# AdaLN FFN on one core: tile 2's experts through ScalarE and VectorE, tile 3's blocks through GpSimd, three convolutions in a row, input 3 issued without a wait

## The reference, cut to what matters

```python
att = softmax(gelu(gelu(c @ W0 + b0) @ W1 + b1) @ W2 + b2)        # 32 x 8
agg_w = einsum('bk,koi->boi', att, weight)                        # one 128x128 matrix per tile
y = einsum('boi,bih->boh', agg_w, x) + (att @ bias_k)[:, :, None] # the "convolution"
qg, sg = dynamic_quant(y * inv_gate); qu, su = dynamic_quant(y * inv_up)   # by row maximum
gate = (qg @ w_gate.T) * sg * s_wgate; up = (qu @ w_up.T) * su * s_wup     # 2048 -> 1024
inter = clip(silu(gate) * up, -10, 10)
qi, si = dynamic_quant(inter * inv_inter)
out = x + (qi @ w_down.T) * si * s_wdown                          # 1024 -> 2048
```

## Time and profile before

| | us |
|---|---|
| median of 3 runs | 804.18 |
| the profiled execution's own time | 804.37 |
| its span in the trace | 802.6 |
| TensorE busy with matmuls | 793.7 |
| VectorE busy | 716.2 |
| ScalarE busy | 441.0 |
| GpSimd busy | 146.1 |

### The profile page before, as it was taken

The page is one execution under the profiler, slowest core; times in us unless marked ns, Lnnn a source line. Parts: engine busy times, 40 slices in busy tenths (PEclk is TensorE's granted clock), DMA queues, the critical chain, the costliest instruction groups (busy, mean ns, idle before and its releaser), DMA issues.

```text
span 802.6 us, 9187 instructions
## 1 busy us (share of the span) xinstructions
PE 793.7 (99%) x3521; PEld 365.1 (45%) x3521; DVE 716.2 (89%) x810; ACT 441.0 (55%) x385; POOL 146.1 (18%) x138
## 2 busy tenths in 40 slices
PE   8999999999999999999999999999999999999997
PEld 4554444444444444444444444444444444444443
DVE  6987899999888998888998888998888988888968
ACT  6774335556664545654555654555654546655531
POOL 2603210210122220122220222210222210222000
PEclk9999999999999999999999999999999999999999
DMA  9997745554445444445444455445455544354342
GB/s 298 241 216 154 163 135 179 146 170 124 127 145 171 145 145 123 120 151 169 146 145 118 118 158 164 150 145 111 120 163 159 156 136 128 107 168 153 94 108 105
DMA packets 162964, 119.81 MB, mean 149 GB/s; under 512 B 151780, under 2 KB 152164, under 8 KB 153703
## 3 DMA queue, kind: packets, MB, share of 16 engines
q1 hardware_dynamic: 161192, 106.64, 44.7%
q0 software_dynamic: 1728, 12.58, 7.7%
HBM read 60.48 MB, written 33.55 MB: 117 GB/s over the span
## 4 chain that ended last, share of the span: by engine, by line
PE 91%; DVE 6%; ACT 2%; issue 1%; DMA 0%; DVEq 0%; ACTq 0%
PE gate_ps L614 26%; PE up_ps L614 26%; PE down_ps L717 23%; PE conv_ps L567 12%; DVE amax L1093 1%; PE gate_ps L717 1%; ACT y L810 0%; DVE region L1165 0%; PE down_ps L572 0%; DVE down_sc L1257 0%; DVE xt L1266 0%; DVE part_max L1172 0%; PE conv_ps L572 0%; ACT wd L810 0%; DVE region L1111 0%
## 5 line engine op out<-in xcount | busy, mean ns | idle before, releaser
L717 PE MATMUL down_ps<-wd,qiT 128*128 128x512 bf16 x896 | 211.2, 379 | 0.0
L614 PE MATMUL gate_ps<-wg,qgT 128*128 128x512 bf16 x928 | 205.7, 379 | 0.0
L614 PE MATMUL up_ps<-wu,quT 128*128 128x512 bf16 x896 | 202.4, 379 | 0.0
L1093 DVE TENSOR_REDUCE amax<-region 128x1 f32<-128x2048 f32 (+1 forms) x90 | 173.1, 1923 | 1.2
L442 POOL TENSOR_TENSOR prod<-wexp,att_bc 128x1024 f32<-128x1024 f32 x28 | 53.1, 1896 | 540.2 <-DVE region L1151 498.5
L717 PEld LDWEIGHTS down_ps<-wd,qiT 128*128 128x128 bf16 x896 | 87.5, 98 | 123.4 <-issue 29.1
L614 PEld LDWEIGHTS gate_ps<-wg,qgT 128*128 128x128 bf16 x928 | 90.7, 98 | 109.5 <-issue 1.1
L614 PEld LDWEIGHTS up_ps<-wu,quT 128*128 128x128 bf16 x896 | 87.7, 98 | 106.1 <-ACT quT L886 0.4
L821 ACT ACTIVATE qg<-region,recip 128x2048 f16<-128x2048 f32 x30 | 60.1, 2002 | 128.3 <-DVE recip L1103 128.3
L567 PE MATMUL conv_ps<-xt,aggw 128*128 128x512 f32 x244 | 116.3, 599 | 1.4 <-ACT y L810 0.8
L810 ACT ACTIVATE y<-conv_ps,aggb 128x512 bf16<-128x512 f32 x116 | 78.9, 686 | 60.0 <-PE conv_ps L567 55.4
(11 more groups left out here) (180 smaller groups left out, 581.2 us busy)
## 6 DMA issues: line engine op xcount, KB each, us to landing
xt<-x SPq DMA_DIRECT2D x30, 1024.0 KB, 4.8
out<-xt SPq DMA_DIRECT2D x29, 1024.0 KB, 4.0
wg<-w_gateT POOLq DMA_DIRECT2D x4, 1024.0 KB, 20.5
wu<-w_upT POOLq DMA_DIRECT2D x4, 1024.0 KB, 17.2
wd<-w_downT POOLq DMA_DIRECT2D x4, 1024.0 KB, 8.6
xt<-x SPq DMA_DIRECT2D x4, 512.0 KB, 4.7
invg_bc<-inv_gate SPq DMA_DIRECT2D x1, 1024.0 KB, 8.7
out<-xt SPq DMA_DIRECT2D x2, 512.0 KB, 2.9
```

Of the source, the lines that this page charges most:

```text
L614: last = nc.tensor.matmul(acc[:, n * BANK:(n + 1) * BANK], codes[:, k * P:(k + 1) * P], wts[:, k, n * BANK:(n + 1) * BANK], start=(k == 0) ...
L717: last = nc.tensor.matmul(down_bank(t, c), qiT_at(t)[:, k * P:(k + 1) * P], wd[:, k, c * BANK:(c + 1) * BANK], start=(k == ks[0]), stop=(k ...
L1093: nc.vector.tensor_reduce(amax[:, i:i + 1], src, axis=AX.X, op=ALU.max, apply_absolute_value=True).then_inc(max_ready, 1)
```

## The change

Tile 2's matrix is no longer made by TensorE. ScalarE writes eight scaled experts into `prod2` (in the place of the up weights' second chunk, which is not loaded yet), spread between its evictions of conv(0) and one after them, and VectorE adds them pairwise in three operations in the middle of `quant_first`. Tile 3's identity blocks now come from GpSimd, in the place where tile 2's came from. On TensorE conv(2) follows conv(1) at once and conv(3) comes before turn_g(1). Tile 3's result gets a home of its own (`quT`), ScalarE's and VectorE's orders are changed to match, and SyncE's wait ahead of x[3] is gone. The diff, cut to its core:

```diff
@@ homes, banks
-        Y_HOME = [y[:, :], wd_part(0, bf16), wd_part(1, bf16)]
+        Y_HOME = [y[:, :], wd_part(0, bf16), wd_part(1, bf16), quT[:, :]]
-            return Y_HOME[t] if t < EARLY else y[:, :]
+            return Y_HOME[t] if t <= EARLY else y[:, :]
-            return bank(up_ps, c - 2) if t < EARLY and c >= 2 else bank(conv_ps, c % 2)
+            return bank(up_ps, c - 2) if t <= EARLY and c >= 2 else bank(conv_ps, c % 2)
+        prod2 = wu[:, 4:6, :].rearrange("p k i -> p (k i)").bitcast(fp32).rearrange("p (k o) -> p k o", o=P)
@@ SyncE
-            sp.wait_ge(wg_in[0], 16)
             sp.dma_start(xslot(3), x[3, :, :]).then_inc(x_in[3], 16)
@@ GpSimd
-            a = att_bc[:, 2 * K:3 * K].unsqueeze(2).to_broadcast([P, K, P])
-            nc.gpsimd.tensor_tensor(diag_at[2].rearrange("p (k r) -> p k r", r=P),
+            a = att_bc[:, EARLY * K:FIRST * K].unsqueeze(2).to_broadcast([P, K, P])
+            nc.gpsimd.tensor_tensor(diag_at[EARLY].rearrange("p (k r) -> p k r", r=P),
...
+            pool.wait_ge(sum2, 3)
             for i in range(WCH - 1):
                 load(wu, w_upT, i, wu_in)
@@ TensorE, waits
+                    elif t == 2:
+                        pe.wait_ge(sum2, 3)
+                    elif t == EARLY:
+                        pe.wait_ge(agg_out, 1)
...
-                    elif t < EARLY or (t == EARLY and c < 2):
+                    elif t <= EARLY:
                         pe.wait_ge(y_ready, NC * t + c - 3)
...
-                    if t == 0:
-                        pe.wait_ge(agg_out, 1)
-                    elif t == 1:
-                        pe.wait_ge(y_ready, NC * EARLY)
+                    if t == 1:
+                        pe.wait_ge(y_ready, NC * FIRST)
@@ TensorE, order
             conv(0)
             conv(1)
-            aggregate_mm(2)
+            conv(2)
             turn_g(0, range(1))
-            aggregate_mm(3)
+            aggregate_mm(EARLY)
             gate(0, range(4))
             turn_g(0, range(1, 2))
-            conv(2)
+            conv(EARLY)
             turn_g(1)
             gate(0, range(4, 8))
             gate(1, HALVES[0])
-            conv(3)
             gate(0, range(8, 12))
@@ ScalarE
-                    elif t == EARLY:
-                        act.wait_ge(xg_ready, 1)
-                        act.wait_ge(xu_ready, 1)
...
+            def experts2(ks):
+                for k in ks:
+                    nc.scalar.activation(prod2[:, k, :], wexp[:, k, :], ACT.Copy, scale=att_col(2, k)).then_inc(scaled2, 1)
...
+                elif t == 2:
+                    act.wait_ge(xu_ready, FIRST)
...
-            conv_out(0)
+            experts2(range(4))
+            conv_out(0, range(1))
+            experts2(range(4, 6))
+            conv_out(0, range(1, 2))
+            experts2(range(6, 7))
+            conv_out(0, range(2, NC))
+            experts2(range(7, K))
             conv_out(1)
+            conv_out(2, range(1))
             quant_g_first(0)
-            aggregate_out(2)
+            conv_out(2, range(1, 2))
+            quant_g_first(1)
             turned_g(0, range(1))
-            quant_g_first(1)
-            aggregate_out(3)
+            aggregate_out(EARLY)
+            conv_out(2, range(2, NC))
             turned_g(0, range(1, 2))
             quant_g(1)
-            conv_out(2, range(2))
-            turned_g(1, range(1))
-            conv_out(2, range(2, NC))
-            turned_g(1, range(1, 2))
+            conv_out(EARLY)
+            turned_g(1)
+            quant_g(2)
             quant_u(0)
-            conv_out(3)
-            quant_g(2)
@@ VectorE
+            def experts2_sum():
+                dve.wait_ge(scaled2, K)
+                nc.vector.tensor_tensor(prod2[:, 0:4, :], prod2[:, 0:4, :], prod2[:, 4:8, :], ALU.add).then_inc(sum2, 1)
+                dve.wait_ge(sum2, 1)
+                nc.vector.tensor_tensor(prod2[:, 0:2, :], prod2[:, 0:2, :], prod2[:, 2:4, :], ALU.add).then_inc(sum2, 1)
+                dve.wait_ge(sum2, 2)
+                nc.vector.tensor_tensor(aggw2, prod2[:, 0, :], prod2[:, 1, :], ALU.add).then_inc(sum2, 1)
...
+                    if c == 1:
+                        experts2_sum()
...
             quant_first()
-            diagonals(3)
             quant_g(1)
+            quant_g(2)
             quant_u(0)
-            quant_g(2)
             quant_u(1)
```

More of the change, by code:

```diff
@@ L145, in adaln_ffn @@
         ones = qiT[:, 0:2 * P].bitcast(fp32)
+        aggw2 = qiT[:, 4 * P:6 * P].bitcast(fp32)
         filler = region1[:, 0:(P + BANK) // 2].bitcast(bf16)
@@ L159, in adaln_ffn @@
         SPLIT = 5
-        diag_at = [region2[:, I:H], prod_flat, region2[:, I:H], prod_flat]
+        diag_at = {0: region2[:, I:H], EARLY: region2[:, I:H]}
+        prod2 = wu[:, 4:6, :].rearrange("p k i -> p (k i)").bitcast(fp32).rearrange("p (k o) -> p k o", o=P)
         def diag_part(t, k):
@@ L186, in adaln_ffn @@
         log_ps = [up_ps[:, 0:FIRST * K], up_ps[:, BANK:BANK + (B - FIRST) * K]]
-        agg_ps = {0: gate_ps[:, BANK:BANK + P], 2: gate_ps[:, BANK:BANK + P], 3: down_ps[:, BANK + P:BANK + 2 * P]}
+        agg_ps = {0: gate_ps[:, BANK:BANK + P], EARLY: down_ps[:, BANK + P:BANK + 2 * P]}
         gturn_ps = down_ps[:, :].bitcast(fp16)
@@ L245, in adaln_ffn @@
         diag_act = sem("diag_act")
-        diag_dve = sem("diag_dve")
+        scaled2 = sem("scaled2")
+        sum2 = sem("sum2")
         diag_pool = sem("diag_pool")
@@ L309, in last_half, with aggw_at @@
             return bank(up_ps if h else down_ps, 1 - h)[:, 0:BANK // 2]
+        def aggw_at(t):
+            return aggw2 if t == 2 else aggw[t % 2][:, :]
         def xcols(t, c):
@@ L530, in aggregate_mm @@
                     pe.wait_ge(wexp_in, 16)
-                elif t == 2:
+                else:
                     pe.wait_ge(diag_pool, 1)
-                else:
-                    pe.wait_ge(diag_dve, 1)
                 for k in ks:
@@ L550, in conv @@
                         pe.wait_ge(agg_sum, 1)
-                    elif t < POOLED:
-                        pe.wait_ge(agg_out, t - 1)
+                    elif t == 2:
+                        pe.wait_ge(sum2, 3)
+                    elif t == EARLY:
+                        pe.wait_ge(agg_out, 1)
                     else:
@@ L566, in conv @@
                         pe.wait_ge(y_ready, NC * t + c - 1)
-                    nc.tensor.matmul(conv_bank(t, c), aggw[t % 2][:, :], xcols(t, c),
+                    nc.tensor.matmul(conv_bank(t, c), aggw_at(t), xcols(t, c),
                                      start=True, stop=True).then_inc(conv_done, 1)
@@ L585, in turn_g @@
                         pe.wait_ge(gcodes_ready, 1)
-                        pe.wait_ge(agg_out, 2)
+                        pe.wait_ge(agg_out, 1)
                     turn(gturn_ps[:, h * I:(h + 1) * I], qg, KI, h * KI, gturn_mm)
@@ L808, in conv_out @@
                     act.wait_ge(conv_done, NC * t + c + 1)
-                    norm = erec[:, t:t + 1] if t < 2 else 1.0
+                    norm = erec[:, t:t + 1] if t < EARLY else 1.0
                     nc.scalar.activation(y_at(t)[:, c * BANK:(c + 1) * BANK], conv_bank(t, c), ACT.Identity,
@@ L840, in aggregate_out @@
             def aggregate_out(t):
-                act.wait_ge(agg_mm, t)
-                act.wait_ge(conv_done, NC * (t - 1))
+                act.wait_ge(agg_mm, 2)
+                act.wait_ge(conv_done, NC * 2)
                 nc.scalar.activation(aggw[t % 2][:, :], agg_ps[t], ACT.Copy, scale=erec[:, t:t + 1]).then_inc(agg_out, 1)
```

6 lines of the change are left out of this document (removed).

## The result

The changed kernel takes 809.59 us (median of 6 runs, 808.6 to 812.96) against 804.16 (6 runs, 804.01 to 804.37): a ratio of 1.0073, 95% interval 1.0062 to 1.0084. It is 5.4 us slower. The forecast had the sign and the mechanism of the start, 3.0 us of the size, and a range that ended at 809.1. The profiled execution is the median one, 809.59 with a span of 807.8.

What follows compares the result with a forecast made beforehand. TensorE bounds the kernel, busy 793.7 of 802.6 us. Idle of 3.75 and 2.33 added, 2.52 and about 0.5 taken away: +3.07 on 804.37 gives 807.4, median 0.2 lower, 807.2; range 804.7 to 809.1.

Steps and rivals of the forecast that it cites:

- conv(2) behind x[2]: Start of TensorE: conv(2) could start at 17.95 but x[2] lands at 21.7, a new idle of 3.75 us.
- x[3]: Ahead of conv(3): x[3] lands at 32.0, between 30.6 and 33.7, a second new idle of 2.33 us.
- The gain of 2.52 on TensorE: Ahead of the first transposition: tile 2's block sums, 1.95 us, and 0.57 of idle behind them go.
- so VectorE's delay is hidden: VectorE's later quantizations, up scales at 39.1 and 44.0, cost TensorE nothing; some 2 us without that cover.
- Whatever shift stands at 38.50 us [...] I expect to stand at the end too: From gate(0)'s third part on, TensorE has no idle to give back, so the +3.07 us reaches the end.
- The clock falls in the idle: Rival: conv(2) runs at the low clock after its idle, 1.2 us remain: 808.4, up to 809.5; chance 0.08.
- x[3] no earlier than before: Rival: the removed wait did not hold x[3]; conv(3) starts at 33.7, shift 4.8, 808.9 us; chance 0.14.
- Faster: Rival: x[2] and x[3] both in time, no new idle, gain 2.52 less some 0.6, 802.3 us; chance 0.10.

Runs made afterwards that it cites:

- e2: The changed kernel with x[3] issued ahead of the four row transfers; 812.46 us.
- e4: The changed kernel with tile 0's up quantization ahead of tile 2's gate quantization again, on VectorE and ScalarE; 810.28 us.
- e7: The kernel before with only SyncE's wait ahead of x[3] taken out; 804.33 us.
- e9: e4 with 44 small matmuls into an unused bank between conv(1) and conv(2); 811.36 us.
- e10: e4 with small matmuls in both waits, 44 ahead of conv(2) and 40 ahead of conv(3); 810.65 us.
- e12: The kernel before with tile 2's matrix by ScalarE and VectorE and tile 3's blocks on GpSimd, convolutions in the old order; 805.99 us.
- e14: The changed kernel with tile 3's gate product moved ahead of tile 1's up half on VectorE; 811.07 us.
- e8: e4 with the gate weights issued at x[1]'s landing and GpSimd making tile 3's blocks ahead of that issue; 805.45 us.
- e1: The changed kernel with SyncE's wait ahead of x[3] put back; 810.65 us.
- e3: The changed kernel with the gate weights issued when x[1] has landed, in place of x[0]; 809.52 us.
- e13: e8 with the change's own order of quantizations, tile 2's gate half ahead of tile 0's up half; 807.41 us.
- e11: e8 with one tiny spread at the start of GpSimd's block and the large spreads held for tile 1's gate product; 817.59 us.

## Why the prediction was wrong, step by step

**conv(2) behind x[2]:** right, and the size partly by luck. The idle is 3.58 us for 3.75 forecast, but x[2] landed at 22.37 for 21.7 and conv(1) ended 0.9 later too: the two halves of conv(0) took 3.75 and 2.36 us in place of 2.98 and 1.88, as it ran longer at the lower clock level, the one of the 1193 ns in the earlier trace rows.

**x[3]:** right. It lands at 32.09 for 32.0. A hit of 0.1 between bounds 3.1 apart is partly luck, though the reason given for the choice holds: e2 shows that the place behind the rows cost x[3] 3.4 us. The wait is 1.56 for 2.33, as conv(2) had started 0.7 later; what counts is the landing. With the same issue it came between 32.07 and 32.38 in six profiles (the change, e4, e7, e9, e10, e12) and at 33.36 in e14, where the rows landed late too (21.87 for 21.12); the forecast's bounds hold both.

**The gain of 2.52 on TensorE:** the changed kernel doesn't test it. gate(0)'s third part stands 9.61 us behind the start of conv(3) (9.57 forecast), and that start is x[3]'s landing, whatever was taken out before it: hence a shift of 3.24 for 3.07. The text called the block sums a gain "if every operand is there in time". e12 shows that the operand behind them, tile 0's codes, was not: taken out alone in that way they gained nothing. Only conv(2) in their place, with its input there, can cash them in (e8: third part at 36.86).

**"so VectorE's delay is hidden":** this is the step that failed. The scale of tile 0's up codes was put at 39.1 us and came at 40.9; tile 1's was put at 44.0 and came at 47.9. Two things were missed. The product of tile 2 started at 30.18, 1 us later than forecast, and took 3.23 rather than the 2.29 that the 4.9 of a quantization had in it. That was to be read before: the same product took 3.25 there (31.32), so that this quantization was 5.87 long (31.32 to 37.19). In both kernels it runs beside a row spread of GpSimd, here this one:

```profile
28.94 2.46 POOL L458 PARTITION_BROADCAST swd_bc<-wu  x2
```

And tile 1's up half can't start before ScalarE has read tile 0's from the same region, a wait of 2.07 that the old order hid behind tile 2's gate half. I then compared the delay with turn_u(0), and with VectorE's slack of 1.35, but the chain ends in `gate_out(0)`, behind one more product. The price on TensorE was 0.96 of idle, 1.1 of shift; e4, with the two quantizations in the old order, has no idle there. The text had named some 2 us if the cover were gone.

**"Whatever shift stands at 38.50 us [...] I expect to stand at the end too":** off by 2.0 us: 1.1 by the step above, 0.5 near 170 us, 0.35 in the last tile. The last appears in every kernel with the new path, e12 among them, as a wait of 0.33 or 0.34 for VectorE's first down output of a late tile, and not before or in e7; VectorE's up output of that tile already stands 0.35 late (769.94 against 764.71, a shift of 5.23 where TensorE's is 4.88). I did not find its cause, nor that of the whole step near 170 us, so that the failed step is about half of what the forecast lacked, and the rest stays open.

**The rivals.** "The clock falls in the idle" was given 0.08 and a price of 1.2. It isn't in the profiled execution of the change, but it is in those of e1, e2 (twice), e3, e4, e9, e13 and e14, each time in or just behind an idle of 2.6 to 3.9 us, at up to 1.7 us each, and twice in e11's behind idles of 5.5 and 4.5. The mean granted clock of the change's runs was 0.996 to 0.999; the slowest run (812.96) has the lowest. It is the likeliest reason for a spread of 4.4 us where the kernel before has 0.4 in its six runs, and for e4's median, though a mean clock doesn't say where it fell. It wanted a larger chance and an upper end near 812. "x[3] no earlier than before" nearly comes about in e14's profiled execution (33.36), not in the change's. "Faster" had its turning point at a landing of x[2] near 20.3 and of x[3] by 28.9; e3 has both (16.07 and 20.84) and was 0.6% slower. For gate(0)'s third part the reasoning was near: e8 has it 1.64 us ahead, for 1.9 forecast (2.52 less 0.6). For the kernel it was false, since VectorE came next, in the forecast's own failed step.

## What to carry to other kernels

When work on the bounding engine is taken out, look first at what stood right behind it and what that waits for: here 1.95 us of block sums filled a wait for codes; taking them out alone put TensorE 0.54 us back in the start and made the kernel 1.7 us slower. When the order of tiles changes on one engine, follow the other engines' chains to their last member before the bounding engine needs them, with each buffer's reader in the chain; one instruction moved into a hole of 2.07 us was worth 3.2 us, half of it because the idle that it removed also cost the clock. An idle of 3 us on TensorE should be priced twice: by its length, and by a slow stretch that may follow. In the 16 profiles the clock fell at ten of the twelve idles of 2.6 to 5.5 us; it cost nothing where a further wait took it in, and up to 1.7 us where none did.

## What was not expected of the hardware

**GpSimd pays at each change of kind.** Between its elementwise product and the spread over partitions stand 9.1 to 11.8 us in which it waits for nothing shown, in both directions (e11). In the kernel before the trace puts 8.72 us in that place on the rows' transfer. In e2, where the rows land at 29.34, the first spread starts 0.14 us behind them: the gap runs beside such a wait and is not added to it.

**A VectorE operation with two inputs waits for GpSimd.** The 512-column sum took 2.98 us beside GpSimd's product and 0.69 alone. The Trainium skill, SBUF — State Buffer, section SBUF: two separate sides, says that of a VectorE operation with two SBUF inputs and a GpSimd operation that reads SBUF the one that starts first has the shared ports for its whole instruction, and the other blocks. e3 and e8 agree that the two don't run together. Which was first they don't settle: by the profile the sum started at 15.79 and the product at 16.26, yet the sum was the one that waited.

**Row transfers ahead of a large input delay its landing.** x[3] landed at 32.09 behind the four rows (e2 has them behind it: 28.69).

**A transposition by DMA took longer where instruction packets fell into it:** 3.6 to 3.7 us without, 4.0 to 4.6 with one, 5.9 with two, in 16 profiled executions. It is observed, not tested.
